# A perceiver block on one core: the 257th key's merge and the softmax division inside the cross-attention loop, one iteration late

## The reference

```
x = x + cross(layernorm(x), ctx, mask)       # 16 heads, 257 keys a batch, masked keys at -1e9, softmax, then Wo
x = x + self(layernorm(x))                   # rotary, 16 query heads on 4 key heads, 32 keys a batch
out = x + mixture(layernorm(x))              # 8 experts, router with a capacity, 128 -> 256 -> 128 with gelu
```

## Time and profile before

| | |
|---|---|
| median of three runs | 739.07 us (738.2 to 739.26) |
| the profiled execution | 739.76 us, its span 737.6 us |
| granted TensorE clock, mean share of full speed | 0.962 |
| busy share of the span | PE 92%, DVE 80%, ACT 68%, POOL 56% |
| transfers on SP's queue in the loop | 512 of CX, 32 KB each; 128 of MK, 128 KB each |

### The profile page before, as it was taken

One profiled execution on the slowest core, in us unless ns is written; L12 is line 12 of the kernel. 1 busy time (PEld: TensorE's weight loads), 2 busy tenths in 40 slices (PEclk: granted clock), 3 DMA queues, 4 the chain that ended last, 5 costly groups with the idle time before them and its releaser, 6 DMA issues.

```text
span 737.6 us, 29041 instructions
## 1 busy us (share of the span) xinstructions
PE 679.4 (92%) x9915; PEld 528.6 (72%) x9915; DVE 590.9 (80%) x1396; ACT 500.6 (68%) x1561; POOL 414.4 (56%) x435
## 2 busy tenths in 40 slices
PE   4999999999999999999999955899999859999994
PEld 2577777777777777777777745777777638888894
DVE  6688888888888888888888768488888866779484
ACT  2788888888888888888888734355555445545552
POOL 4675636456364554636364278377777658207375
PEclk9999999999999999999999989599999859999998
DMA  8444444444444444444448173000000020003721
GB/s 180 96 85 88 89 85 88 90 93 92 90 89 87 92 92 94 91 86 89 88 83 137 23 219 91 2 4 5 1 0 2 3 72 1 1 3 107 230 77 41
DMA packets 186526, 55.05 MB, mean 75 GB/s; under 512 B 146708, under 2 KB 184856, under 8 KB 186466
## 3 DMA queue, kind: packets, MB, share of 16 engines
q1 hardware_dynamic: 182768, 49.74, 31.7%
q0 software_dynamic: 1824, 3.96, 1.6%
q10 hardware_dynamic: 1874, 0.54, 0.4%
HBM read 44.51 MB, written 8.83 MB: 72 GB/s over the span
## 4 chain that ended last, share of the span: by engine, by line
PE 85%; DVE 6%; POOL 3%; issue 2%; ACT 2%; DMA 1%; POOLq 0%; DVEq 0%; ACTq 0%
PE bank L499 39%; PE energy L499 24%; PE bank L502 22%; POOL SX L945 1%; POOL TQ L937 1%; DVE stats L1526 1%; DVE STAT L1580 1%; DMA X<-in_x 1%; PE energy L502 1%; ACT PR L647 0%; POOL COEF L930 0%; POOL out L1028 0%; DVE xn L1509 0%; DVE stats L1677 0%; DVE mv L1489 0%
## 5 line engine op out<-in xcount | busy, mean ns | idle before, releaser
L647 ACT ACTIVATE PR<-energy,STAT 128x256 f32<-128x256 f32 x512 | 234.8, 484 | 53.8 <-DVE STAT L1580 53.7
L1580 DVE TENSOR_REDUCE STAT<-energy 128x512 f32 (+1 forms) x256 | 164.5, 685 | 45.2 <-PE energy L499 45.2
L502 PE MATMUL bank<-ident,PR 128*128 128x128 f32 x1024 | 158.9, 281 | 0.6 <-DVE PT L1594 0.5
L502 PEld LDWEIGHTS bank<-ident,PR 128*128 128x128 f32 x1024 | 111.6, 141 | 60.5 <-ACT PR L647 31.2
L1594 DVE COPY PT<-bank 128x512 f32<-128x512 f32 x192 | 126.2, 684 | 11.5 <-PE bank L502 9.5
L841 POOL TENSOR_TENSOR QB<-QT,headmask 128x512 f32<-128x512 f32 x32 | 33.3, 1040 | 160.5 <-DMA MK<-in_mask_BxSxS_ik 110.5
L647 ACT ACTIVATION_READ_ACCUMULATOR PR<-energy,STAT (+1 forms) x512 | 110.4, 216 | 0.0
L848 POOL TENSOR_SCALAR MZ<-MK 128x512 bf16<-128x512 int32 x64 | 94.2, 1488 | 7.4 <-DMA MK<-in_mask_BxSxS_ik 7.4
L499 PEld LDWEIGHTS bank<-PT,VT 128*32 128x32 f32 x2048 | 53.1, 109 | 23.1 <-issue 22.5
L499 PE MATMUL bank<-PT,VT 128*32 128x128 f32 x2048 | 69.2, 275 | 0.3
L499 PE MATMUL bank<-wv_s,CT 128*128 128x128 f32 x512 | 67.8, 275 | 0.5 <-issue 0.5
(11 more groups left out here) (270 smaller groups left out, 1333.6 us busy)
## 6 DMA issues: line engine op xcount, KB each, us to landing
CX<-in_ctx SPq DMA_DIRECT2D x512, 32.0 KB, 2.5
MK<-in_mask_BxSxS_ik SPq DMA_DIRECT2D x128, 128.0 KB
rows_in<-fill SPq DMA_DIRECT2D x1, 3483.0 KB, 19.8
X<-in_x SPq DMA_DIRECT2D x4, 512.0 KB, 7.5
VLT<-v_last SPq DMA_DIRECT2D x4, 512.0 KB, 9.6
PAY<-rows_in SPq DMA_DIRECT2D x2, 903.0 KB, 7.2
PAY<-X SPq DMA_DIRECT2D x1, 1280.0 KB, 6.8
w_s<-in_L_ffn_W SPq DMA_DIRECT2D x1, 1024.0 KB, 5.6
```

The costliest lines, as they stand in the source:

```text
L502: return nc.tensor.transpose(o, i, ident[0:n, 0:n])
L647: nc.scalar.activation(PR[:, b, g, :], EB[:, g, e * KEYS:(e + 1) * KEYS], ACT.Exp, bias=STAT[:, bass.ds(t, 1), b, 1, g:g + 1].rearrange("p ...
L1580: V.tensor_reduce(STAT[:, bass.ds(t, 1), b:b + 2, 1, g:g + 1].rearrange("p a b g -> p (a b g)"), EB[:, g, :].rearrange("p (e k) -> p e k", ...
```

## The change

- **Half banks.** DVE takes minima in five operations instead of four: of the first batch in banks 0 and 1 (`first_minimum`, 256 columns each), of both batches in banks 2 and 3, and of the second batch in banks 0 and 1 (`second_minimum`, after two exponentials). Exponentials, turns and copies go by units of two halves: (batch 0: banks 0, 1), (bank 2), (bank 3), (batch 1: banks 0, 1). The energies' semaphore counts twice in a step.
- **The merge in the loop.** Iteration v is 8 batches. DVE does its merge in iteration v+1: gaps at r = 0, totals and reciprocal at r = 1, two coefficients and a turn of 128 x 64 at r = 2; ACT does one exponential of 128 x 64 at r = 1. SP sends the turned coefficients to DRAM and, an SP iteration later, loads them spread over the head's channels (COEFS, one buffer, four transfers). POOL then multiplies OT by one coefficient, the last value (VLD, now turned, channels by batches) by the other, and adds.
- **Flags.** MK is loaded with all 257 columns; POOL takes the 257th's flags in two small operations per pair. Last energies are formed at step 1 and turned at step 2; both late query groups are projected in step 0.
- **Behind the loop** stay the gaps, totals and coefficients of the last iteration, the sends and spreads of the last iterations, and out-projection, residual and statistics straight from OT.
- **W1H and W1L** are made in eight parts in self-attention steps 4 to 11.

The diff, cut to its core:

```diff
@@ SP
+            def send_coefficients(v):
+                sp.wait_ge(m_turned, v + 1)
+                sp.dma_start(coef_rows[bass.ds(v, 1), :, :].rearrange("a p c -> p (a c)"), COEFT[:, :]).then_inc(st_cf, 16)
+            def spread_coefficients(v):
+                sp.wait_ge(st_cf, 16 * v + 16)
+                wait_reuse(sp, pool_t1, v)
+                for g in range(NG):
+                    sp.dma_start(COEFS[32 * g:32 * g + 32, :, :, :].rearrange("p n w q -> p (n w q)"),
+                                 coef_rows[bass.ds(v, 1), :, :].rearrange("a (h g n) c -> g h a (n c)", h=4, g=NG)[g]
+                                 .broadcast_to([4, HD, 16 * SQ])).then_inc(ld_cf, 16)
-            with sp.Fori(1, NP // 4) as i:
+            with sp.Fori(1, 3) as i:
                 for k in range(4):
                     load_pair(i * 4 + k, k, False)
+            for i in (3, 4):
+                for k in range(4):
+                    load_pair(i * 4 + k, k, False)
+                send_coefficients(i - 3)
+                if i > 3:
+                    spread_coefficients(i - 4)
+            with sp.Fori(5, NP // 4) as i:
+                for k in range(4):
+                    load_pair(i * 4 + k, k, False)
+                send_coefficients(i - 3)
+                spread_coefficients(i - 4)
+            spread_coefficients(NV - 4)
+            send_coefficients(NV - 3)
             for dst, src in small_s:
...
+            spread_coefficients(NV - 3)
+            for v in (NV - 2, NV - 1):
+                send_coefficients(v)
+                spread_coefficients(v)
             sp.wait_ge(ev_o, NP)
@@ ACT
+            def gap_exponents(v):
+                act.wait_ge(m_diff, 2 * v + 2)
+                nc.scalar.activation(GAP[:, :, :], GAP[:, :, :], ACT.Exp).then_inc(m_exp, 1)
...
+                if r == 1 and not (start and p < 4):
+                    gap_exponents(i - 1)
+                for u in range(4):
+                    exponents(i, r, u)
@@ POOL
+            def weigh_out(v):
+                pool.wait_ge(ld_cf, 16 * NG * v + 16 * NG)
+                pool.wait_ge(pool_o, 2 * v + 2)
...
+                nc.gpsimd.tensor_tensor(out_t(2 * P * v), out_t(2 * P * v), COEFS[:, :, 0, :], ALU.mult).then_inc(pool_w, 1)
+                nc.gpsimd.tensor_tensor(COEFS[:, :, 1, :], COEFS[:, :, 1, :], VLD[:, bass.ds(8 * v, 8)].rearrange("p (n a) -> p n a", a=1)
+                                        .broadcast_to([P, 8, SQ]), ALU.mult).then_inc(pool_w, 1)
+                pool.wait_ge(pool_w, 2 * v + 2)
+                nc.gpsimd.tensor_tensor(out_t(P * (2 * v + 1) - P), out_t(P * (2 * v + 1) - P), COEFS[:, :, 1, :], ALU.add).then_inc(pool_t1, 1)
+            with pool.Fori(4, NT // 2) as i:
+                for k in range(2):
+                    tile(i, k, False)
+                weigh_out(i - 4)
             pool.wait_ge(ld_s, N_S)
...
+            weigh_out(NV - 4)
+            keep_own(NT - 3, (NT - 3) % 2)
+            weigh_out(NV - 3)
+            keep_own(NT - 2, (NT - 2) % 2)
+            weigh_out(NV - 2)
+            keep_own(NT - 1, (NT - 1) % 2)
+            weigh_out(NV - 1)
@@ PE
             def out_project(u, j):
-                pe.wait_ge(dve_otn, u + 1)
+                pe.wait_ge(pool_t1, 2 * u + 2)
@@ DVE
+            def coefficients(v, part):
...
+                elif part == 2:
+                    dve.wait_ge(m_own, 6 * v + 6)
+                    wait_reuse(dve, st_cf, 16 * v)
+                    V.transpose(COEFT[:, :], COEF[:, :, :].rearrange("p w n -> p (w n)")).then_inc(m_turned, 1)
+            def merge(i, r, part):
+                if r == 3:
+                    if part == 0:
+                        last_energy(i)
+                elif not (static(i) and i == 0):
+                    (gaps, totals, coefficients)[r](i - 1, part)
...
                     evac_turned(i, r, 0)
+                    merge(i, r, 0)
                     evac_turned(i, r, 1)
+                    merge(i, r, 1)
                 if not (start and p + 3 >= NP):
                     turn_context(i, r + 3)
+                if not last:
+                    merge(i, r, 2)
```

More of the change, by code:

```diff
@@ L674, in _ @@
             evac_k(0, 1)
-            act.wait_ge(vl_ok, 1)
-            act.dma_start(v_last, VL[:, :]).then_inc(st_vl, 16)
             step_range(act, step)
             evac_third(NP // 4, -1)
[L681 to L706, removed]
+            gap_exponents(NV - 1)
             act.wait_ge(lg_tr, 1)
@@ L1094, in energies, with turn @@
                                   KS[rows, k % 2, cols], start=False)
[L1095 to L1097 removed]
+                        if e == 1 and g in (0, NG - 1):
+                            last.then_inc(pe_s, 1)
+            def turn(i, r, u):
                 p, k, t = pair(i, r)
[L1099 to L1101 removed]
+                pe.wait_ge(act_exp, 8 * p + (2 * u + 2))
+                if u:
+                    wait_reuse(pe, ev_t, 3 * p + u - 1)
                 else:
                     wait_reuse(pe, ev_u, p)
[L1104 removed]
+                if isinstance(p, int) and (p, u) == (0, 1):
+                    pe.wait_ge(n0_qt, LATE_Q + 2)
+                if isinstance(p, int) and (p, u) == (2, 0):
+                    pe.wait_ge(el_ok, 2)
+                for n, (e, g) in enumerate(UNITS[u]):
                     for j in range(KC):
[L1106 to L1107 removed]
+                        col = (n * KC + j) * P
+                        last = tr(psum[1 if u % 2 else 7][:, col:col + P],
                                   PR[:, 2 * (k % 2) + e, g, j * P:(j + 1) * P])
@@ new lines, in totals @@
+            def totals(v, part):
+                if part == 0:
+                    dve.wait_ge(m_exp, v + 1)
+                    V.tensor_tensor(by_group(SUM[:, :]), by_group(GAP[:, 0, :]), own_stats(v, 0), ALU.mult)\
+                        .then_inc(m_own, 1)
+                elif part == 1:
+                    dve.wait_ge(m_own, 6 * v + 3)
+                    V.tensor_tensor(SUM[:, :], SUM[:, :], GAP[:, 1, :], ALU.add).then_inc(m_own, 1)
+                else:
+                    dve.wait_ge(m_own, 6 * v + 4)
+                    V.reciprocal(SUM[:, :], SUM[:, :]).then_inc(m_own, 1)
@@ L1624, in _ @@
             step_range(dve, step)
-            dve.wait_ge(pe_el, 2)
-            dve.wait_ge(mlb_ok, 1)
-            for k in range(4):
-                V.tensor_tensor(ELAST[:, k, :, :],
-                                psum[0].rearrange("p (i g k) -> p k i g", i=NT, g=NG)[:, k],
-                                MLB[:, :].rearrange("p (i a) -> p i a", a=1).broadcast_to([P, NT, NG]),
-                                ALU.add).then_inc(dve_c, 1)
-            chain[0] += 4
-            dve.wait_ge(dve_c, chain[0])
@@ L1660, in _ @@
-            dve.wait_ge(x_biased, 1)
-            def add_last(u, j):
-                dve.wait_ge(pool_t1, u + 1)
-                dve.wait_ge(pe_rb, u + 1)
-                wait_reuse(dve, pe_x1, u - 1)
-                V.tensor_tensor(OTP[:, 2 + j, :, :].rearrange("p n k -> p (n k)"),
-                                OTP[:, j, :, :].rearrange("p n k -> p (n k)"), psum[j], ALU.add).then_inc(dve_otn, 1)
+            for part in range(3):
+                gaps(NV - 1, part)
+            step(NP // 4, 0)
@@ L1669, in cross_residual @@
+            for part in range(3):
+                totals(NV - 1, part)
+            for part in range(3):
+                coefficients(NV - 1, part)
+            evac_out(NP // 4, -1)
+            dve.wait_ge(x_biased, 1)
             def cross_residual(u, j):
```

367 lines of the change are left out of this document (172 added, 195 removed).

## The result

The changed kernel takes **773.03 us** (median of 4 runs, 771.74 to 776.19) against 738.63 of the kernel before on the same chip: a ratio of 1.0457, 95% interval 1.0431 to 1.0484. Slower was forecast, at 761 within 738 to 779. The profiled execution took 771.74 us with a span of 769.8; the one before 739.76 with 737.6.

What follows compares the result with a forecast made beforehand. PE was full and SP's queue issued with 6% to spare; five added transfers would make SP the pace. Moments 22.6 us later took the profiled 739.76 to 762.4, the median 0.7 below, given as 761 us; range 738 to 779.

Steps and rivals of the forecast that it cites:

- SP's queue as the pace: In the loop, one send and four spreads add 3.6 us of SP issue; an iteration becomes 26.84 us, over 24.7 of computing.
- The tail: From the last MK's issue to the moments' end: SP and POOL wait for each other, 59.5 us, ending at 483.2.
- Product 12: POOL's product behind the loop, after copies of 2.2 us, itself 2.2 us, ending at M + 31.7.
- M: Time by which SP has issued the last MK load, forecast at 423.7 us against 385.6 before.
- the three rounds: Behind product 12: gap and three spread issues 2.3, fourth's landing 3.4, product 2.2, so 7.9 us each, to M + 55.4.
- The spreads' landing: In each round of the tail, 3.4 us, taken from v_last's same 64 KB; ends 2.5 (CX) and 5.2 (MK).
- DVE's wait: DVE's coefficient turn waits for the previous send, first at step 10; stalls of 2 us an iteration, adding nothing to M.
- The last energies: PE's last energies move from the final two steps to step 1, turn in step 2: at most 3 us, covered by SP.
- Half banks at 0: First exponential waits for 256 columns' minimum; possible gain 0.3 us a step, 19 over 63 steps, entered as 0.
- Issue hidden: Rival: the five transfers cost SP nothing, M is 384.1, moments end at 443.6, time 722 us; chance 0.12.
- Short tail: Rival: SP paces the loop, but POOL's and SP's rounds overlap more, some 20 us less tail, 741 us; chance 0.07.
- Clock: Rival: PE's clock falls in the stalls, 30% of time at 1.2 GHz, 29.1 us an iteration, 789 us; chance 0.09.

## Why the prediction was right, and where it was not

**SP's queue as the pace: right, the term too small.** The forecast step is "one send (0.2 gap + 0.48) and four spreads (0.3 gap + 4 x 0.66, priced as MK)", 3.6 us. Measured between 157.01 and 161.26: 0.28 + 0.39 + 0.35 + 3.23 = 4.25. The spreads are the mis-sized part, 0.81 each instead of 0.66; the loop written out shows 0.65, what I had assumed, so the price was right for the transfer and wrong for a transfer in this loop. An iteration came to 27.5 instead of 26.84, and the last MK to 432.09 instead of 423.7: 0.9 before iteration 4, 0.7 in it, 7.1 in the ten that follow, -0.2 in the last.

**The tail: right as a sum, in part by luck** (61.6 from the last MK, forecast 59.5). Product 12 ended at M + 30.1 (forecast 31.7); the three rounds took 26.6 (23.7), two of them 7.9 and 8.0 as forecast and the last 10.7, its spreads landing beside the weights' loads and the fill; from there 4.9 (4.1), as PE at half its clock (0.50 in 488 to 490) took 2.08 us for the last out-projection (1.16 in the earlier trace rows). The 1.6 us gained ahead of the rounds cancel part of the 3.7 lost in and behind them. The spreads' landing, 3.4 in the sum, shows as 3.5 and 3.8 in the first two rounds (from the start of the fourth issue to POOL's product). By the Trainium skill's rule (DMA: Bandwidth & Descriptors, Rules for kernel authors) I had put it near MK's 5.2, and that estimate is not borne out here; on how many engines the spreads ran, no view shows, and MK against CX was a weak hint, since MK moves 128 KB and CX 32.

**DVE's wait: right in place and in being no price of its own.** Behind the first it is 1.5 to 3.3 us an iteration, 2.7 on average, about what SP takes over the computing; taking it away did not change the time, though it brought the loop's end 7.9 us forward. The first was forecast at 12 and came to 4.7, for a reason I had not seen:

**The last energies: wrong, and hidden.** I gave them "at most 3 us, covered because SP paces those steps too". In the changed kernel the keys of step 5 come at 61.84 instead of 52.13: 9.7 us. PE's rows show three parts there: the row of short matmuls (6.55 us), the turn in step 2 (2.02 us), and a clock that fell after the row's gaps. PE in 40 to 46 us, in the changed kernel and then in the kernel before (columns as in the earlier trace rows):

```profile
40.00:42.00 2.00, 0.16 (x12) 0.16 (x16) 0.00 (x0) 0.46 (x3) 2.00 (x1) 0.70 0.35 65
42.00:44.00 2.00, 2.00 (x53) 1.82 (x50) 0.92 (x2) 0.00 (x0) 2.00 (x1) 0.50 0.40 56
...
42.00:46.00 4.00, 4.00 (x50) 3.09 (x40) 3.79 (x8) 3.53 (x16) 3.89 (x1) 1.00 0.32 82
```

The cover held (SP's iteration 4 was 0.9 us late), so nearly nothing of it is in the result; in the versions whose loop PE paces it stands in the time: 9.0 us with the transfers in ACT's waits, and with the energies in four parts 5.8 (57.88 at step 5) or, at the lower clock, 7.5 (59.65).

**Half banks at 0: right, as far as is shown.** Alone they bring 2.5 us, not the 19 of a third of ACT's wait; the changed kernel without them was not run.

**The rivals.** Issue hidden: false. The Trainium skill's sentence (the same page, Issuing engines are not separate DMA queues) that the time to initiate is usually small beside the transfer speaks of one transfer, and for one it comes out here as a fifth: 0.81 us of issue for a spread that lands 3.5 to 3.8 after its start. My comparison of eight issues with one landing did not test it. What the rows show is that the issues of one queue add up, 3.23 us for four. Short tail: false. Clock: false as the pace (0.99 in 200 to 400); it did fall after PE's waits of 3.73 and 2.25 us, to 0.57 in 112 to 116 and in 218 to 222.

In sum the moments came 10.5 us later than forecast, 8.4 of it at the last MK, most of that from one price on one queue; what follows the moments came out 0.9 shorter, and the median lies 1.3 above the profiled run where I had put it 0.7 below (762.4 less 0.7 is 761.7, not 761). The direction and the mechanism were right, the size was not: 34 us were lost where 22 were forecast, inside the range but in its upper third.

## What to carry to other kernels

Count what each queue issues per iteration as you count an engine's work: here SP had 6% to spare, two more small transfers cost the loop 3 us and five cost it 31 to 44 (with the waits for the sends), on an engine that computes nothing. A transfer moved to a busy engine's queue costs about the same (0.63 to 0.74 us on ACT, 0.66 on POOL) unless it stands where that engine waits anyway; price it from a row with the same shape and the same kind of address. And a cost that another one covers is still to be sized: it is the next bound once the cover goes.

## What the hardware showed that I had not expected

Four spreads whose address comes from a loop register took 3.23 us and 0.69 behind them; written out, 2.60 and 0.04. Plain CX loads went the other way, 3.94 on average for eight in the loop and 4.25 written out. SP's instructions by line split this, in the changed kernel and then written out, both in 160 to 400 us (shortest, median and longest, in ns):

```profile
L543 SPq MOVE COEFS<-coef_rows x33: 29/38/38, 160.5 to 380.8; - x33
L543 SPq DMA_DIRECT2D COEFS<-coef_rows x34: 639/640/697, 159.8 to 380.9; - x34
L524 SPq DMA_DIRECT2D CX<-in_ctx x282: 316/317/729, 162.0 to 399.8; - x141
...
L543 SPq DMA_DIRECT2D COEFS<-coef_rows x36: 597/622/658, 181.9 to 385.7; - x36
L524 SPq DMA_DIRECT2D CX<-in_ctx x309: 437/451/1101, 159.9 to 399.9; - x155
```

A spread's own issue is nearly the same in both, 0.64 and 0.62 us. In the loop register operations stand between the transfers, and the four spreads take 0.67 us more than four times 0.64; written out there are none. A CX load's own issue, though, is shorter in the loop, 0.32 against 0.45 us; why stays open.

A row of 256 short matmuls in step 1 left PE 3.6 us without anything to wait for; laid out in four parts, 2.0.

A DVE operation on 128x32 elements, 0.20 us elsewhere, took 1.01 beside a product of POOL. That the one held up the other is not shown by an edit:

```profile
237.58 1.01 DVE L1642 TENSOR_TENSOR GAP<-LEAST,STAT 128x32 f32<-128x32 f32 x1
```
```profile
237.46 1.05 POOL L875 TENSOR_TENSOR OC<-OC,headmask 128x512 f32<-128x512 f32 x1
```

That is the version with the energies in four parts, in a step 1 of 7.2 us.
